# Two-layer graph network: 20 units of the last row panel lose their product in the first sweep and get it as tiles at the end of the second

## What is computed

```python
a_tilde = adj + eye(N)
d = rsqrt(sum(adj, axis=1) + 1e-6)
h = (d[:, None] * a_tilde * d[None, :]) @ (x @ weight)       # layer 0
x1 = layernorm(x + h)
agg = adj @ x1                                               # layer 1
msg = relu(agg @ W_msg.T + b_msg)
new = gru_cell(msg, x1, W_ih, W_hh, b_ih, b_hh)              # r, z, n gates
out = layernorm(x1 + new)
```

## Time and profile before

| | us |
|---|---|
| median of 3 runs | 1920.8 (1919.12 to 1923.04) |
| the profiled execution | 1920.14 |
| its span, first to last instruction | 1918.1 |
| PE busy | 1704.1 (89%) |
| DVE busy | 1390.7 (73%) |
| ACT busy | 639.0 (33%) |

### The profile page before, as it was taken

How to read it: one execution, slowest core, us unless ns; L and a number is a source line. 1 busy time by engine, 2 the same in 40 slices (tenths; PEclk the granted TensorE clock), 3 DMA queues, 4 the chain that set the end, 5 groups by cost and what they waited for, 6 DMA issues and landing times.

```text
span 1918.1 us, 16476 instructions
## 1 busy us (share of the span) xinstructions
PE 1704.1 (89%) x6384; PEld 1165.4 (61%) x6384; DVE 1390.7 (73%) x1192; ACT 639.0 (33%) x556; POOL 119.6 (6%) x110
## 2 busy tenths in 40 slices
PE   0053949799999999799999999999999999999996
PEld 0032424344454544588888888888777777777774
DVE  5997868968887663386666666655778888878885
ACT  0000000000000000254544444444665666656562
POOL 0000000000000000020000000000001010010101
PEclk9986969899999999899999999999999999999998
DMA  9997989989999783366656666665998889989891
GB/s 391 421 421 327 410 330 413 411 329 421 414 400 348 285 293 121 121 198 200 205 190 195 203 196 194 198 196 192 343 329 297 303 298 309 319 284 319 300 311 59
DMA packets 180925, 551.07 MB, mean 287 GB/s; under 512 B 13424, under 2 KB 13936, under 8 KB 148080
## 3 DMA queue, kind: packets, MB, share of 16 engines
q1 hardware_dynamic: 177280, 541.11, 77.4%
q0 software_dynamic: 2560, 8.39, 1.3%
q10 hardware_dynamic: 1008, 0.53, 0.1%
HBM read 545.79 MB, written 4.19 MB: 287 GB/s over the span
## 4 chain that ended last, share of the span: by engine, by line
PE 77%; DMA 12%; DVE 8%; ACT 1%; issue 1%; SPq 0%; POOL 0%; ACTq 0%; DVEq 0%; POOLq 0%
PE bank L322 22%; PE bank L355 16%; PE bank L357 15%; PE bank L356 15%; DVE colsum L611 5%; DMA ring<-adj_blocks 5%; DMA pool<-adj_blocks 4%; DMA spare<-adj_blocks 2%; DVE lo L620 1%; DMA bhh_s<-b_hh 1%; PE bank L310 1%; ACT hi L508 1%; PE bank L422 1%; PE bank L329 1%; PE bank L435 1%
## 5 line engine op out<-in xcount | busy, mean ns | idle before, releaser
L620 DVE TENSOR_TENSOR lo<-ring,hi 128x2048 fp32r<-128x2048 f32 x204 | 465.5, 2289 | 295.2 <-ACT f L514 224.9
L508 ACT ACTIVATE hi<-ring 128x2048 fp32r<-128x2048 f32 x204 | 391.1, 1918 | 413.6 <-DMA ring<-adj_blocks 269.9
L355 PE MATMUL bank<-hi,x1s 128*128 128x512 f32 x1024 | 417.4, 408 | 6.7 <-DVE x1s L670 3.5
L357 PE MATMUL bank<-hi,x1s 128*128 128x512 f32 x1024 | 399.9, 391 | 0.0
L611 DVE TENSOR_TENSOR colsum<-colsum,kept 128x2048 f32<-128x2048 f32 x115 | 263.6, 2292 | 86.1 <-DMA kept<-adj_blocks 85.3
L356 PE MATMUL bank<-lo,x1s 128*128 128x512 f32 x816 | 318.8, 391 | 0.0
L322 PE MATMUL bank<-kept,feat 128*128 128x512 f32 x664 | 296.5, 598 | 3.8 <-DMA kept<-adj_blocks 3.8
L355 PEld LDWEIGHTS bank<-hi,x1s 128*128 128x128 f32 x1024 | 192.9, 188 | 57.5 <-issue 7.2
L322 PEld LDWEIGHTS bank<-kept,feat 128*128 128x128 f32 x664 | 126.8, 192 | 160.0 <-issue 155.4
L357 PEld LDWEIGHTS bank<-hi,x1s 128*128 128x128 f32 x1024 | 192.7, 188 | 41.3
L484 ACT ACTIVATE dege<-bank 128x8 f32<-128x8 f32 x8 | 1.4, 177 | 568.4 <-PE bank L310 568.4
(11 more groups left out here) (91 smaller groups left out, 1489.3 us busy)
## 6 DMA issues: line engine op xcount, KB each, us to landing
ring<-adj_blocks SPq DMA_DIRECT2D x408, 512.0 KB, 5.4
kept<-adj_blocks SPq DMA_DIRECT2D x120, 1024.0 KB, 10.3
ring<-adj_blocks SPq DMA_DIRECT2D x70, 1024.0 KB, 10.0
pool<-adj_blocks SPq DMA_DIRECT2D x53, 1024.0 KB, 11.6
more<-adj_blocks SPq DMA_DIRECT2D x104, 512.0 KB, 6.0
spare<-adj_blocks SPq DMA_DIRECT2D x13, 1024.0 KB, 18.2
xt<-x_t SPq DMA_DIRECT2D x8, 512.0 KB, 7.5
xin<-x POOLq DMA_DIRECT2D x16, 256.0 KB, 3.6
```

Of the source, the lines that this page charges most:

```text
L355: pe.matmul(acc[:, :], fh, ah, start=start and c == 0, stop=False, skip_group_check=True)
L357: mm = pe.matmul(acc[:, :], fl, ah, start=False, stop=stop and c == KC - 1, skip_group_check=True)
L508: ins = act.activation(hi[:, n % NHI], raw(slot_of2[n]), ACT.Copy)
L620: ins = dve.tensor_tensor(flat(low(n)), flat(raw(slot_of2[n])), flat(hi[:, n % NHI]).bitcast(f32), ALU.subtract)
```

## The change

1. `lower_units(P)`: in panel 7 only units 0 to 7 keep their product (`LAST_LOW = 8`), before it was 0 to 27; units 8 to 27 are now far. The other panels are as before. The list `products` goes from 156 to 136. Five units of panel 7 come before its degrees, three after; slot 12 is last held by unit (7, 31), before by (7, 19).
2. No row is whole any more. Rows 15 and 14 come at the end of the second sweep (`rows2`), with columns 13 to 4 each: 20 tiles more, of both layers.
3. In rows 13 to 0 the tiles of columns 15 and 14 serve layer 0 alone, since x1 of these rows is not known yet (`both`): 28 tiles, which are loaded and split once more in the last stage for layer 1, at the end of each row. The eight of them in rows 13 to 10 come first of all. N2 is 120 instead of 100 (92 tiles of both layers), the last stage has 164 tiles instead of 156, in another order of rows, 284 loads in all instead of 256.
4. `tile_done` becomes `second_done`, and a slot or a hi buffer of a one-layer tile is freed by `first_done` (`tile_used`). `spill` runs for 14 rows (rows 13 and 12 have no layer-1 sums by then).
5. `brz` is made behind the last fold of sweep one; ACT waits for it in `rz_step`.

```diff
+    LAST_LOW = 8
+    LAST = (NT - 2, NT - 1)
 
     def kept_unit(P, j):
         return j // 4 == P or (P in BAND and j // 4 == P + 1)
 
+    def lower_units(P):
+        return list(range(4 * P)) if P < NP - 1 else list(range(LAST_LOW))
+
     def early_unit(P, j):
-        return j // 4 < P or kept_unit(P, j)
+        return j in lower_units(P) or kept_unit(P, j)
 
     def early(i, k):
         return early_unit(i // 2, 2 * k)
 
     def panel_order(P):
-        low = list(range(4 * P))
-        far = [j for j in range(4 * P, NU) if not kept_unit(P, j)]
+        low = lower_units(P)
+        far = [j for j in range(NU) if not early_unit(P, j)]
         kept = [j for j in range(4 * P, NU) if kept_unit(P, j)]
-        head, tail = low[:max(0, 4 * P - LATE)], low[max(0, 4 * P - LATE):]
+        head, tail = low[:max(0, len(low) - LATE)], low[max(0, len(low) - LATE):]
...
-    before_degrees = {P: [j for j in panel_order(P) if j < 4 * P][:max(0, 4 * P - LATE)] for P in range(NP)}
-    after_degrees = {P: [j for j in panel_order(P) if j < 4 * P][max(0, 4 * P - LATE):] for P in range(NP)}
+    before_degrees = {P: lower_units(P)[:max(0, len(lower_units(P)) - LATE)] for P in range(NP)}
+    after_degrees = {P: lower_units(P)[len(before_degrees[P]):] for P in range(NP)}
...
-            if j < 4 * P:
+            if j in lower_units(P):
...
-    whole = [i for i in range(NT) if all(early(i, k) for k in range(NT))]
-    rows2 = [i for i in range(NT - 1, -1, -1) if i not in whole]
-    rows3 = [15, 0, 14, 1, 13, 2, 12, 3, 11, 4, 10, 5, 9, 6, 8, 7]
-    T2 = [(i, k) for i in rows2 for k in range(NT - 1, -1, -1) if not early(i, k)]
+
+
+    rows2 = [i for i in range(NT - 3, -1, -1)] + [NT - 1, NT - 2]
+    rows3 = [13, 0, 12, 1, 11, 15, 10, 14, 9, 2, 8, 3, 4, 5, 6, 7]
+
+    def both(i, k):
+        return not early(i, k) and not (i not in LAST and k in LAST)
+
+    T2 = []
+    for i in rows2:
+        T2 += [(i, k) for k in range(NT - 1, -1, -1) if not early(i, k)]
+
+    T2 = [t for t in T2 if t[0] in (13, 12, 11, 10) and t[1] in LAST] + \
+         [t for t in T2 if not (t[0] in (13, 12, 11, 10) and t[1] in LAST)]
     N2 = len(T2)
     end2 = {i: max(n for n, t in enumerate(T2) if t[0] == i) for i in rows2}
     start2 = {i: min(n for n, t in enumerate(T2) if t[0] == i) for i in rows2}
-    T2 += [(i, k) for i in rows3 for k in range(NT - 1, -1, -1) if early(i, k)]
+    spills = [i for i in rows2 if any(both(i, k) for k in range(NT))]
+    end1 = {i: max(n for n, t in enumerate(T2) if t[0] == i and both(*t)) for i in spills}
+    start1 = {i: min(n for n, t in enumerate(T2) if t[0] == i and both(*t)) for i in spills}
+    for i in rows3:
+        left = [k for k in range(NT - 1, -1, -1) if not both(i, k)]
+        T2 += [(i, k) for k in left if k not in LAST] + [(i, k) for k in left if k in LAST]
     NN = len(T2)
...
-    norm_rows = whole[::-1] + rows2
-    norm_no = {i: q for q, i in enumerate(norm_rows)}
+    norm_no = {i: q for q, i in enumerate(rows2)}
...
+        def tile_used(eng, n):
+
+            if n >= N2 or both(*T2[n]):
+                eng.wait_ge(second_done, second_no[n])
+            else:
+                eng.wait_ge(first_done, n + 1)
...
-                    sp.wait_ge(tile_done, before2[n] + 1)
+                    tile_used(sp, before2[n])
...
-                    pe.wait_ge(evicted, NT)
-                if begin and 2 <= j < len(rows2) + 2:
+                    pe.wait_ge(evicted, NT - 2)
+                if begin and 2 <= j < len(spills) + 2:
                     pe.wait_ge(spilled, j - 1)
-                if begin and j >= len(rows2) + 2:
-                    pe.wait_ge(agg_ready, j - len(rows2) - 1)
+                if begin and j >= len(spills) + 2:
...
-            layer0(0)
-            for i in whole[::-1][:2]:
-                turn(i)
-            layer0(1)
-            layer1(0)
-            for i in whole[::-1][2:]:
-                turn(i)
-            for n in range(1, NN + TAIL):
-                if 2 <= n < N2:
+            for n in range(NN + TAIL):
+                if n < N2:
                     layer0(n)
                 i = normed_row(n, 1)
                 if i is not None:
                     turn(i)
-                if n < NN:
+                if n < NN and (n >= N2 or both(*T2[n])):
...
             def rz_step(i):
+                act.wait_ge(brz_ready, 1)
...
-            split_hi(2)
-            for i in whole[::-1]:
-                x1_hi(i)
-            for n in range(3, NN + TAIL):
+            for n in range(2, NN + TAIL):
                 if n < NN:
                     split_hi(n)
                 i = normed_row(n, 3)
-                if i is not None:
+                if i in spills:
...
-            dve.wait_ge(weights_in, NW * 16)
-            dve.tensor_tensor(brz[:, 0:1], bih_s[:, 0:1], bhh_s[:, 0:1], ALU.add)
-            dve.scalar_tensor_tensor(brz[:, 1:2], bih_s[:, 1:2], -1.0, bhh_s[:, 1:2], ALU.mult, ALU.subtract)\
-               .then_inc(zeroed, 1)
...
+            dve.wait_ge(weights_in, NW * 16)
+            dve.tensor_tensor(brz[:, 0:1], bih_s[:, 0:1], bhh_s[:, 0:1], ALU.add)
+            dve.scalar_tensor_tensor(brz[:, 1:2], bih_s[:, 1:2], -1.0, bhh_s[:, 1:2], ALU.mult, ALU.subtract)\
+               .then_inc(brz_ready, 1)
...
+                acc = acc1[(len(spills) + g) % 2]
+                dve.wait_ge(second_done, second_no[end3[i]])
...
-            first = whole[::-1]
-            split_lo(0)
-            split_lo(1)
-            row_step(first[0])
-            if len(first) > 1:
-                row_step(first[1])
-            x1_step(first[0])
-            x1_lo(first[0])
-            for a, b in zip(first[1:], first[2:]):
-                row_step(b)
-                x1_step(a)
-                x1_lo(a)
-            if len(first) > 1:
-                x1_step(first[-1])
-                x1_lo(first[-1])
-            for n in range(2, NN + TAIL):
+            for n in range(NN + TAIL):
```

More of the change, by code:

```diff
@@ L94, in gnn_resnorm_kernel @@
     start2 = {i: min(n for n, t in enumerate(T2) if t[0] == i) for i in rows2}
-    T2 += [(i, k) for i in rows3 for k in range(NT - 1, -1, -1) if early(i, k)]
+    spills = [i for i in rows2 if any(both(i, k) for k in range(NT))]
[4 more added lines that the diff above has]
+        T2 += [(i, k) for k in left if k not in LAST] + [(i, k) for k in left if k in LAST]
     NN = len(T2)
+    second_no = [sum(n >= N2 or both(*T2[n]) for n in range(m + 1)) for m in range(NN)]
     end3 = {i: max(n for n in range(N2, NN) if T2[n][0] == i) for i in rows3}
@@ L237, in gnn_resnorm_kernel @@
             sem("supp_done"), sem("feat0_ready"), sem("prod_done"), sem("evicted"))
-        hi_ready, lo_ready, tile_done = sem("hi_ready"), sem("lo_ready"), sem("tile_done")
-        first_done, tall_ready, turned = sem("first_done"), sem("tall_ready"), sem("turned")
+        hi_ready, lo_ready, brz_ready = sem("hi_ready"), sem("lo_ready"), sem("brz_ready")
+        first_done, second_done = sem("first_done"), sem("second_done")
+        tall_ready, turned = sem("tall_ready"), sem("turned")
         y_ready, stats_ready, var_ready, veps_ready, rstd_ready = (
@@ L333, in _ @@
             pe.wait_ge(consts, 2)
-            pe.wait_ge(zeroed, 4)
+            pe.wait_ge(zeroed, 3)
             pe.wait_ge(weights_in, NW * 16)
@@ L375, in layer1 @@
                 if n >= N2:
-                    j = len(rows2) + rows3.index(i)
+                    j = len(spills) + rows3.index(i)
                     begin, stop = n == start3[i], n == end3[i]
@@ L379, in layer1 @@
                 else:
-                    j = rows2.index(i)
-                    begin, stop = n == start2[i], n == end2[i]
+                    j = spills.index(i)
+                    begin, stop = n == start1[i], n == end1[i]
                 if begin and j == 1:
-                    pe.wait_ge(evicted, NT)
-                if begin and 2 <= j < len(rows2) + 2:
+                    pe.wait_ge(evicted, NT - 2)
+                if begin and 2 <= j < len(spills) + 2:
                     pe.wait_ge(spilled, j - 1)
-                if begin and j >= len(rows2) + 2:
-                    pe.wait_ge(agg_ready, j - len(rows2) - 1)
+                if begin and j >= len(spills) + 2:
+                    pe.wait_ge(agg_ready, j - len(spills) - 1)
                 pe.wait_ge(x1_whole, norm_no[k] + 1)
                 layer(n, lambda c: (x1s[:, k * KC + c, 0, :], x1s[:, k * KC + c, 1, :]), acc1[j % 2],
-                      begin, stop).then_inc(tile_done, 1)
+                      begin, stop).then_inc(second_done, 1)
             def turn(i):
                 q = norm_no[i]
[L394 to L397, removed]
+                pe.wait_ge(tall_ready, q + 1)
                 if q >= 2:
@@ L400, in turn @@
                 for c in range(KC):
-                    of = part[:, i * W + c * 128:i * W + (c + 1) * 128] if i in whole else tall[:, c * 128:(c + 1) * 128]
```

(26 more changed lines are left out.)

## The result

| | before | after |
|---|---|---|
| median, us | 1921.92 (1919.12 to 1926.45) | 1951.92 (1949.85 to 1953.22) |
| profiled execution, us | 1920.14 | 1950.87 |
| its span, us | 1918.1 | 1948.7 |

The ratio is 1.0153, with a 95% interval of 1.013 to 1.0176: 1.5% slower, 30.0 us by the medians and 30.6 by the spans. The forecast was +18.9 us; direction and range held, the size was short by about 11 us.

What follows compares the result with a forecast made beforehand. PE was taken as the bound after 812 us, with almost no waits; -43.7 + 16.3 + 40.8 + 4.0 + 1.5 = +18.9 us gave 1939.7, say 1940 us, 1.0% slower, range 1929 to 1960 us.

Steps and rivals of the forecast that it cites:

- Who bounds what: From 812 us on, PE sets the end: nearly every matmul added or removed moves it by its length.
- End of sweep one: Panel 7: the column sum replaces PE as pace setter, fold at 707.9 us, burst ends at 739.7, 43.7 us earlier.
- Start of sweep two: After the burst: ACT and DVE are the path, ten layers take 44.5 us against 28.2 for five, +16.3 us.
- the clock: Single tiles at the beginning of sweep two: matmuls run slow after PE's waits, as seven did before, +1.5 us.
- Rival 1: Sweep two's single tiles: slow clock throughout makes PE the bound, 57 us instead of 44.5, 1952 us; chance 0.10.
- Row starts: Sweep two, rows 9 to 0: PE waits 0.4 us for the third tile, ten times, +4 us, bounds 0 to 15.
- the feature copy: Third tile of rows 9 to 0: its feature copy waits for the first single layer, PE waits 0.4 us.
- Last stage: Third stage: extra loads and splits of 28 tiles stay hidden, ratio kept at DMA 0.89, counted as 0 us.
- Gate bias: Head: DVE no longer waits 20.4 us, panel 0's fold at 92.8 not 95.6, then DMA decides, 0 us.
- Rivals 2 to 5: Panel 7's sum starves, +21.6 us, 0.09; head counts, 1919.6, 0.06; layer cheaper, 1917, 0.01; panel 7 stays PE-bound, no chance given.

## Why the forecast was right, and where it was short

**Who bounds what.** Right. With 14 and with 20 low units what lies behind the burst became shorter by 2.65 and 2.64 us for each layer less, against 2.72 from the earlier trace rows; with 16 it was 26.7 us for eight, of which 7.4 are the better start. The 28 more loads and splits show only as waits: with the one-layer tiles spaced out, 202 layers of sweep two took 555.9 us, 6.5 more than their work, where 195 layers before took 7.5 more. The sentence "From 700 us on PE is busy in every slice" passes over 750 to 800 us, where PE waited at the start of sweep two.

**End of sweep one.** Right in the mechanism, and to 2 us in the place: the fold ended at 709.8 (forecast 707.9), the burst at 742.2 (739.7). 1.3 of the 2.5 us had been there since panel 4, 0.7 is that the three products stayed slow a little longer (13.3 instead of 12.6). PE's idle time ahead of the fold is 10 us (forecast 11), and there are 8.8 us more ahead of the fifth product, at 685 to 693.7 us, where it waits for a load; the sum ends later, so they cost nothing; the slow clock behind it, 3.57 us for the degree column, came as the earlier trace rows had it.

**Start of sweep two.** Mis-sized: 48.4 us for ten layers, forecast 44.5 and 1.5 for the clock. The failing term is the clock. I took the seven slow matmuls of the earlier trace rows; behind the 5.53 us wait the whole first layer was slow, 5.3 us instead of 2.7, and ACT's and DVE's next steps hang on that layer, so that the third tile slipped with it, and the fifth, whose load waits for the first tile's slot. Seven slow matmuls more, behind the 2.52 us wait at 780.8, cost PE 1.5 us that nothing takes up again; those at 771 us lie beside the chain of work, which runs over DVE there. 2.6 and 1.5 are 4.1 us where I had 1.5, and that is the 2.4 us by which the stage missed. Rival 1, the slow clock through all single tiles, did not happen: the clock was 0.90 in 750 to 800 us, with the slow level in three stretches of it, and matmuls were 0.23 us apart in between. That its 1952 us is what was measured is chance: the other 9 us lie in the other lines of the table.

**Row starts.** Mis-sized by half: 12 waits of 0.44 (forecast ten of 0.4) but 8 to 9 us with what a restart costs. The reason that I gave, the feature copy, holds in part: it is seen at five of the ten places. The slot's round trip lies so close behind it that it decides at the others and takes over when the order changes; only the order that answers both took the waits away.

**Last stage.** I counted 0, it cost 2.4 us: at its beginning PE waits 2.0 us for a lo and eight matmuls behind that are slow (before: 1.5 us and none slow).

**Gate bias.** Right: nothing within what can be measured. The fold of panel 0 ended at 91.9 us (forecast 92.8), panel 1's degree column began at 173.5.

**Rivals 2 to 5.** The sum did not starve for slots: units of panel 7 were summed every 2.49 us, DMA at 1.01. The head did not count. A layer was not cheaper than the trace says: 0.227 us a matmul, 448 of them in 900 to 1000 us of the experiment with one-layer tiles three places apart. The figure of about 131 ns in the Trainium skill (TensorE: Matmul & The Clock Gate, "Back-to-back issue gap") is met nowhere here. The change does what it says.

## What to carry to other kernels

Work moved out of a bound stage gains only until the next resource of that stage sets its pace; the number to move is the one at which both end together (here 12 units, the best of the four numbers tried, not 20), and past it each piece costs nearly its full price elsewhere. With a ring of buffers, compare the time of the consumer over the items between with the whole round trip of a slot; short items then have to be spread so far that no window of that length holds two. Look at which buffer holds the last item of a stage: the first item of the next stage may wait for just that one.

## What was unexpected of the hardware

- Short waits of PE were followed by the slow level: with 14 low units, behind a wait of 3.5 us, the degree column took 3.58 us, as behind a wait of 45.6 us (3.57); with 16 units and no wait it took 1.68. In the changed kernel matmuls 0.43 us apart stood behind waits of 2.7, 2.5 and 2.0 us (at 770.8, 780.8 and 1367.0), and none behind one of 1.4 us (at 765.0).
- A wait that the profile gives as 0.44 us cost PE's stream about 0.7 us.
- The small operations on POOL between statistics and normalization vary in the records: 0.19 and 1.03 us at 797 us before, 2.15 and 1.36 for the first row after (767 us). DVE waits for them 0.3 us at each of two places among the single tiles.
